# A graph attention layer with a top-2 mixture of experts on one core: GpSimd normalises rows, expert rows are cleared step by step, and the last matrix, the routing and the y store are reordered

## What is computed

```python
def layernorm(x): return (x - mean(x)) / sqrt(var(x) + 1e-5)

q, k, v = (layernorm(x) @ W.T + b for W, b in ((Wq, bq), (Wk, bk), (Wv, bv)))
x = x + softmax(q @ k.T / sqrt(256) + adj + adj) @ v

xf = layernorm(x)
probs = softmax(xf @ router_w + router_b)              # 1354 x 8
topk_p, topk_i = top_k(probs, 2); gates = scatter(topk_p at topk_i)
h = einsum("td,edh->teh", xf, w1) + b1                 # H = 512
gated = silu(h @ wg + bg) * (h @ wv + bv)              # per expert, 512 x 512 each
y = gated @ w2 + b2                                    # 512 x 256 per expert
x = x + einsum("ted,te->td", y, gates)
```

## Time and profile before

| | us |
|---|---|
| median of 3 runs | 450.05 (449.73 to 450.64) |
| the profiled execution | 449.44 |
| its span | 447.7 |

### The profile page before, as it was taken

The page is one execution under the profiler, slowest core; times in us unless marked ns, Lnnn a source line. Parts: engine busy times, 40 slices in busy tenths (PEclk is TensorE's granted clock), DMA queues, the critical chain, the costliest instruction groups (busy, mean ns, idle before and its releaser), DMA issues.

```text
span 447.7 us, 8184 instructions
## 1 busy us (share of the span) xinstructions
PE 390.6 (87%) x2272; PEld 334.7 (75%) x2272; DVE 322.1 (72%) x737; ACT 185.7 (41%) x332; POOL 269.0 (60%) x293
## 2 busy tenths in 40 slices
PE   0887998199999999999999974999888989999981
PEld 0776877089988888988988753788776878888870
DVE  3665879946978988898896987376554756777664
ACT  1574574145455365455545351362222223333320
POOL 3053689835538656755855861666887480377772
PEclk9988999689999999999999996899999999999996
DMA  8761447055666567477266657754564641233235
GB/s 247 259 229 53 141 130 258 33 160 158 208 177 183 190 201 239 145 214 257 98 204 240 266 191 222 280 193 152 215 229 170 245 169 59 84 96 96 68 117 178
DMA packets 44861, 78.94 MB, mean 176 GB/s; under 512 B 5278, under 2 KB 25186, under 8 KB 43796
## 3 DMA queue, kind: packets, MB, share of 16 engines
q1 hardware_dynamic: 32916, 64.87, 43.2%
q10 hardware_dynamic: 9280, 8.00, 5.6%
q0 software_dynamic: 2624, 5.56, 4.1%
HBM read 56.13 MB, written 22.29 MB: 175 GB/s over the span
## 4 chain that ended last, share of the span: by engine, by line
PE 44%; DVE 15%; DMA 14%; issue 9%; POOL 5%; ACT 4%; ACTq 3%; DVEq 2%; SPq 2%; POOLq 1%
PE ps L978 21%; PE ps L1279 9%; DMA expert_out<-ysum 6%; DVE acc L1391 5%; PE ps L1176 4%; DMA xblk<-expert_rows 2%; DMA first_row<-in_L_ffn_bv 2%; DMA wq_raw<-in_L_gnn_Wq 2%; PE ps L1124 2%; PE ps L1178 2%; DVEq L340 2%; DVE ps L1705 2%; POOL picked L704 1%; DMA picked<-expert_out,ypos_i 1%; POOL lo L597 1%
## 5 line engine op out<-in xcount | busy, mean ns | idle before, releaser
L597 POOL TENSOR_TENSOR lo<-raw,hi 128x512 fp32r<-128x512 f32 x60 | 76.0, 1297 | 59.0 <-DVE acc L1391 55.4
L1279 PE MATMUL ps<-weights,bT_hi 128*128 x232 | 72.4, 393 | 0.0
L978 PE MATMUL ps<-hi,w1T_lo 128*128 128x512 f32 x128 | 55.8, 436 | 17.1 <-DVE w1T_lo L1332 10.3
L978 PE MATMUL ps<-hi,w1T_hi 128*128 128x512 f32 x128 | 53.0, 414 | 0.0
L978 PE MATMUL ps<-lo,w1T_hi 128*128 128x512 f32 x128 | 52.6, 411 | 0.0
L1279 PE MATMUL ps<-weights,bT_lo 128*128 x116 | 48.8, 420 | 3.8 <-ACT silu L952 3.1
L1279 PEld LDWEIGHTS ps<-weights,bT_hi 128*128 128x128 f32 x232 | 43.8, 189 | 7.5
L1176 PE MATMUL ps<-v,pT_hi 128*128 128x256 f32 (+3 forms) x242 | 44.7, 286 | 0.0
L978 PEld LDWEIGHTS ps<-hi,w1T_lo 128*128 128x128 f32 x128 | 25.8, 202 | 23.0 <-DVE w1T_lo L1332 10.5
L1279 PE MATMUL ps<-weights,gT_hi 128*128 x232 | 42.9, 283 | 0.0
L1391 DVE SCALAR_TENSOR_TENSOR acc<-raw,b1T,acc 128x512 f32<-128x512 f32 x48 | 41.4, 862 | 1.5
(11 more groups left out here) (222 smaller groups left out, 994.5 us busy)
## 6 DMA issues: line engine op xcount, KB each, us to landing
raw<-in_L_ffn_wg SPq DMA_DIRECT2D x8, 1024.0 KB, 6.3
raw<-in_L_ffn_wv SPq DMA_DIRECT2D x8, 1024.0 KB, 6.5
products<-ring SPq DMA_DIRECT2D x28, 256.0 KB, 4.0
landed<-products SPq DMA_DIRECT2D x7, 1024.0 KB, 7.2
adj_sb<-in_adj SPq DMA_DIRECT2D x10, 677.0 KB
bias<-biases SPq DMA_DIRECT2D x8, 640.0 KB, 5.5
w1raw<-in_L_ffn_w SPq DMA_DIRECT2D x8, 512.0 KB, 5.1
landed<-in_L_ffn_w SPq DMA_DIRECT2D x8, 512.0 KB, 4.2
```

The source lines that it names most:

```text
L597: G.tensor_tensor(lo[j % RAWS][:, k, :], raw[j % RAWS][:, k, :], r32(hi[j % HIS][:, k, :]), ALU.subtract).then_inc(m_lo, 1)
L978: last = nc.tensor.matmul(o, a, b, start=begins and n == 0, stop=ends and n == len(m) - 1)
L1279: last = nc.tensor.matmul(o, stationary[i][:, k, :], part(e, ats[j] + k * width, width), start=n == 0, stop=n == len(m) - 1)
```

## The change

What it does, in the order of the program:
- The factors of all tiles are computed in one go on VectorE after all statistics. Rows of tiles 0 and 1 stay on ScalarE, those of tiles 2 to 10 go to GpSimd. The rest of `wqk` is computed ahead of the tile loop, one `turn_w1` stands ahead of the wait for it. SyncE waits for the query and key matrices before it loads w1 and raw. `gather_bias(0)` is in one piece and `multiply(0, 0)` goes chunk by chunk.
- `gather_bias(3)` stands inside step 1, behind the first two rests of the transposed probabilities; the load of `first_row` 4 stands behind a raw load. L1549 is a TENSOR_SCALAR in place of a TENSOR_TENSOR. GpSimd adds the value bias to x one tile a step. The copy of the normalised tile (`xn2_copy`) is gone, TensorE reads it where it is.
- In each of the eleven steps SyncE clears 128 rows of each of the eight experts (1 MB); the eight clears after the steps are gone, and a scatter waits for its step's clear.
- The bias sums of matrices 14 and 15 are split and begun earlier, matrix 15's ahead of the last `add_mix`; its lo is made by GpSimd (two chunks) and by VectorE ahead of the tables; routing and ranking stand elsewhere between the product chunks; block 0 is loaded from row 0 without the table; VectorE's rest of block 0 stands inside the tables.
- In an expert block ScalarE copies gT before it stores y and loads rows; y sums have three buffers in place of two.

```diff
-    ROWS = 4
+    ROWS, YSUMS = 4, 3
...
-    FACTORS = [(0, 2 * PER), (2 * PER, TILES - 2 * PER)]
+    FIRST = 2
...
+            sp.wait_ge(wqk_in, 48)
             load_w1(0)
             load_raw(0)
             load_first_row(0)
...
+            def clear_rows(t):
+
+                if t > 0:
+                    sp.wait_ge(rows_cleared, 16 * t)
+                sp.dma_start(xs.rearrange("(e c p) d -> p c e d", e=E, p=P)[:, t, :, :],
+                             zeros[:, :].rearrange("p (a d) -> p a d", a=1).broadcast_to([P, E, D])
+                             ).then_inc(rows_cleared, 16)
...
-                if s + 4 < MATS:
+                if 0 < s and s + 4 < MATS:
                     load_first_row(s + 4)
                 store_product(2 * j + 1)
                 if j + RAWS < MATS:
                     load_raw(j + RAWS)
+                if s == 0:
+                    load_first_row(s + 4)
...
+                if s < TILES:
+                    clear_rows(s)
...
-            sp.wait_ge(ends_done, 1)
-            clear_ends(0, padded[0])
-            clear_ends(E // 2, padded[1])
             load_bias(0)
+            load_weights(2)
+            load_down(2)
             store_bias_row(TILES + 3)
             store_product(2 * TILES + 6)
+
+            sp.wait_ge(scattered, 16 * TOPK * TILES)
+            sp.dma_start(xblk[:, 0, :], xs[0:P, :]).then_inc(rows_in[0], 16)
             store_product(2 * TILES + 7)
-            sp.wait_ge(padded[0], 16 * (E // 2))
             sp.wait_ge(rows_done, 1)
-            sp.wait_ge(scattered, 16 * TOPK * TILES)
-            for i in range(3):
+            for i in range(1, 3):
                 row = sp.value_load(at(block_row[0:1, :], i), min_val=0, max_val=E * REGION - P)
                 sp.dma_start(xblk[:, i, :], xs[bass.ds(row, P), :]).then_inc(rows_in[i], 16)
-            load_weights(2)
-            load_down(2)
             load_bias(1)
             store_product(2 * MATS - 2)
+            store_bias_row(MATS - 1)
             load_bias(2)
             store_product(2 * MATS - 1)
-            store_bias_row(MATS - 1)
             sp.wait_ge(tables_done, 1)
             for e in range(SLOTS, E):
...
+                pool.wait_ge(rows_cleared, 16 * (t + 1))
...
-            finish_factors(pool.wait_ge, G, 1, pool)
+            def x_rows(t):
+                w = width(t)
+                G.tensor_scalar(xn2_all[:w, t, :], x1[:w, t, :], rs[:w, 1, t:t + 1], rs[:w, 3, t:t + 1],
+                                ALU.mult, ALU.add).then_inc(xn_last_done, 1)
+
+            pool.wait_ge(factors_done, 1)
+            for t in range(FIRST, TILES):
+                x_rows(t)
...
-            for t in range(TILES):
+            for t in range(2):
...
+                if s + 1 < TILES:
+                    add_bv(s + 1)
                 if 0 <= s - 4:
                     count_tile(s - 4)
                     scatter(s - 4)
             count_tile(TILES - 3)
-            scatter(TILES - 3)
+
+            pool.wait_ge(m_hi, MATS)
+            pool.wait_ge(acc_done, KH * (MATS - 1) + 2)
+            for k in range(2):
+                chunk_lo(MATS - 1, k)
             count_tile(TILES - 2)
-            scatter(TILES - 2)
-            scatter(TILES - 1)
-            sum_lo(MATS - 1)
...
+            product_lo(0)
             pool.wait_ge(tables_done, 1)
-            for e in range(E):
+            down_lo(0)
+            for e in range(1, E):
...
-            x_rows(0)
-            x_rows(1)
+            for t in range(FIRST):
+                x_rows(t)
             act.wait_ge(small_done, 1)
             copy(wvT[0][:, :, D:VW], bk_turned[:, :, :]).then_inc(wvT_hi, 1)
-            x_hi(0)
-            x_rows(2)
-            x_hi(1)
             act.wait_ge(wqk_mm, 1)
             copy(wqk[0][:, :, :], ps[:, 4:7:2, 0:D]).then_inc(wqk_hi, 1)
-            x_rows(3)
+            x_hi(0)
+            x_hi(1)
             for t in range(TILES):
                 if t + 2 < TILES:
                     x_hi(t + 2)
                 v_part(t)
-                if t + 4 < TILES:
-                    x_rows(t + 4)
                 if t == 2:
-                    w1_hi(0, 0, 4)
-                    w1_hi(0, 1, 5)
+                    w1_hi(0, 0, 5)
+                    w1_hi(0, 1, 4)
...
-                if s == 1:
-                    sum_hi(3)
                 keep_bias_row(j, MIX)
                 matrix_hi(s + 3)
                 keep_product(2 * j)
                 pT_part(s - 1, 2)
                 if s + 1 < TILES:
                     q_part(s + 1)
-                if 0 <= s - 2:
-                    xn2_copy(s - 2)
+                if s == 1:
+                    sum_hi(3)
                 sum_hi(s + 3)
                 w1_hi(j // 2 + 1, j % 2, COMB)
                 if s < TILES:
                     probabilities(s)
+                else:
+                    xn2T_part(TILES - 2)
                 keep_product(2 * j + 1)
...
-            xn2T_part(TILES - 2)
             matrix_hi(MATS - 1)
+            xn2T_part(TILES - 1)
             keep_bias_row(LATE, MIX)
-            xn2_copy(TILES - 1)
             w1_hi(LATE // 2 + 1, LATE % 2, COMB)
-            xn2T_part(TILES - 1)
+            keep_product(2 * LATE)
             sum_hi(MATS - 1)
-            keep_product(2 * LATE)
+            keep_product(2 * LATE + 1)
             down_hi(0)
-            keep_product(2 * LATE + 1)
             keep_bias_row(LATE + 1, MIX)
             slot_hi(1)
             keep_product(2 * LATE + 2)
             down_hi(1)
+            keep_product(2 * LATE + 3)
...
+                if 0 <= s - 1 < BLOCKS:
+                    act.wait_ge(gT_mm, s)
+                    if s >= 3:
+                        act.wait_ge(y_mm, s - 2)
+                    copy(gT[(s - 1) % 2][0][:, :, :], by_k(ps[:, BANK_GT[(s - 1) % 2], :], KH)).then_inc(gT_hi, 1)
                 if 0 <= s - 3 < BLOCKS:
                     b = s - 3
                     act.wait_ge(y_sum, b + 1)
                     if b > 0:
                         act.wait_ge(y_out, 16 * b)
-                    act.dma_start(ys[span(b, P), :], ysum[:, b % 2, :]).then_inc(y_out, 16)
+                    act.dma_start(ys[span(b, P), :], ysum[:, b % YSUMS, :]).then_inc(y_out, 16)
                 if s + 3 < BLOCKS:
                     load_rows(s + 3)
-                if 0 <= s - 1 < BLOCKS:
-                    act.wait_ge(gT_mm, s)
-                    if s >= 3:
-                        act.wait_ge(y_mm, s - 2)
-                    copy(gT[(s - 1) % 2][0][:, :, :], by_k(ps[:, BANK_GT[(s - 1) % 2], :], KH)).then_inc(gT_hi, 1)
...
-                pe.wait_ge(xn_done, t + 1)
-                if t >= 2:
+                if t < FIRST:
+                    pe.wait_ge(xn_done, t + 1)
+                else:
+                    pe.wait_ge(xn_last_done, t - FIRST + 1)
                     pe.wait_ge(xT_lo, t - 1)
...
-                pe.wait_ge(m_lo, KH * (j + 1))
+                pe.wait_ge(m_lo, KH * j + chunks[-1] + 1)
...
+                    turn_w1(0, 0, 5)
                     pe.wait_ge(wqk_lo, 1)
-                    turn_w1(0, 0, 4)
-                    turn_w1(0, 1, 5)
+                    turn_w1(0, 1, 4)
                 if t == 3:
                     queries(0)
                 if t == 6:
-                    multiply(0, 0)
+                    for k in range(KH):
+                        multiply(0, 0, range(k, k + 1))
...
             route(TILES - 2)
+            turn_xn2(TILES - 1)
             multiply(LATE, 0, range(KH // 2))
-            turn_xn2(TILES - 1)
+            route(TILES - 1)
             multiply(LATE, 0, range(KH // 2, KH))
             rank(TILES - 2)
-            route(TILES - 1)
-            multiply(LATE, 1)
+            multiply(LATE, 1, range(KH - 1))
             rank(TILES - 1)
+            multiply(LATE, 1, range(KH - 1, KH))
...
+            pe.wait_ge(prod_done, 2 * LATE + 1)
+            for k in range(KH):
+                multiply(LATE + 2, 0, range(k, k + 1))
             pe.wait_ge(bias_row_done, LATE + 2)
             sum_bias(LATE + 2, MIX)
-            pe.wait_ge(prod_done, 2 * LATE + 1)
-            multiply(LATE + 2, 0)
...
-            statistics(0)
-            statistics(1)
-            rough_factors(0)
-            finish_factors(dve.wait_ge, V, 0, dve)
+            for g in range(len(GROUPS)):
+                statistics(g)
+            factors()
...
+            dve.wait_ge(wqk_hi, 1)
+            sub(wqk[1][:, :, :], ps[:, 4:7:2, 0:D], r32(wqk[0][:, :, :])).then_inc(wqk_lo, 1)
             for t in range(TILES):
                 if t + 2 < TILES:
                     x_rest(t + 2)
                 v_rows(t)
-                if t == 0:
-                    statistics(2)
-                    rough_factors(1)
                 if t == 1:
-                    dve.wait_ge(wqk_hi, 1)
-                    sub(wqk[1][:, :, :], ps[:, 4:7:2, 0:D], r32(wqk[0][:, :, :])).then_inc(wqk_lo, 1)
```

(48 more changed lines are left out.)

101 lines of the change are left out of this document (43 added, 58 removed).

## The result

The changed kernel takes 442.43 us (median of 4 runs, 441.74 to 442.77) against 450.02 for the kernel before; the ratio is 0.9828, 95% interval 0.9811 to 0.9845. The forecast was 425.6, with 415 to 437: the sign was right, the gain 7.6 us where 24.4 were forecast. The gain is clear of the noise, but under 2%. The profiled execution has a span of 439.8 us (before 447.7).

A forecast was written before the change was run, and what follows sets the result against it. TensorE alone was taken to bound the nine steps, so gains lie in holes outside them: 7 + 9.4 + 0 + 3 + 5 = 24.4 off 449.4, plus 0.6 for the median: 425.6 us, range 415 to 437.

The forecast's parts named there:

- the factors then end at 13.57 + 1.4 = 15.0: First stage: adding the third group's statistics on VectorE delays all row factors by 1.4 us, to 15.0.
- the four bias sums are issued together: First stage: helps remove TensorE's 2.85 us wait for GpSimd's lo of the first matrix; VectorE's longer block costs some 0.7.
- rival D: Step 1: another wait, the query rest and then the residual sum, replaces L1549's; 3 us earned, not 9.4; 432; chance 0.1.
- short hole: Step 1: a short TensorE wait ahead of the product's second half at 80.0, partly half clock, ending at 83.5.
- rival E: Nine steps: the 1 MB clears make them DMA-bound if each costs above 9.3 us; say 453; chance 0.03.
- rival C: After the steps: the first row of matrix 15 isn't held, so no 5 us TensorE stand; 420.5; chance 0.15.
- GpSimd now issues three tiles' back to back, until 269.9: After the steps: GpSimd's last scatters, three tiles' in a row, are all issued by 269.9, ahead of the first block's load.
- landing 5 later: After the steps: the last scatters land 5 us after issue, and the first block is then loaded, at 277.7.
- VectorE's remaining tables: After the steps: 4.4 us of tables behind VectorE's new wait for the first block, behind the lower bound of -3.
- Rivals A: First stage: GpSimd's new burst blocks VectorE's 0.15 us bias instruction until 24 to 26; stage -1, not 7; 433.6; chance 0.14.
- B: Expert blocks: the store reordering earns nothing, as the row loads behind the stores become late; 431; chance 0.12.
- F: First stage and end: chunked product and early rest find other operands late; together they earn 2; 433.5; chance 0.06.

The follow-up runs named there:

- the seven repairs: Changed kernel with third-group statistics and matrix 0's bias sums split, matrix 4's first row loaded earlier, plus the four repairs behind the steps: 428.61 us, ratio 0.9559.
- the four repairs: Changed kernel with matrix 15's first bias sums, third expert's weights and VectorE's first-block lo later, third-last tile's scatter earlier: 436.99 us, ratio 0.9729.

## Why the prediction was wrong

**First stage, 7 forecast, 0.8 measured.** The step that failed is "the factors then end at 13.57 + 1.4 = 15.0". It counted the added work and took its data as there. In the kernel before, the statistics of the third group ran at 20.29, and no row told when that part of x had landed; it was 12.04, with VectorE idle ahead. The trace of before held a hint: its statistics start at 5.3 and 8.6 us, each released by the landing of its group, so an estimate by the same spacing puts the third group at 11.9. The wait was to be "just covered" up to 16.3; the factors came at 16.64, and the half clock made 1.3 us late into 4.1 by 24.5. The run with the statistics split off gives 5.0 for this cause. The second failure is "the four bias sums are issued together" booked as a gain for the product with 0.7 us of cost; three of them ran at 1.37 us each beside GpSimd, and splitting them gave 2.7. The two don't add up to 7.7, as GpSimd's lo is then the next wait. That GpSimd's rows are hidden was right.

**Step 1, 9.4 forecast, 6.0 measured.** The form of L1549 was right (0.21 us in all steps). The forecast's times are on the clock of the kernel before, 0.8 us later than this trace's; on it the row landed at 72.9 (72.5 forecast), which was right, VectorE's sum behind it ended at 78.4 (76.7), the second half began at 81.6 (80.0) and ended at 86.9 (83.5). So two terms were too small: the sum, whose four instructions took 5.5 us beside GpSimd's subtraction where the forecast left 4.2, and the "short hole", which was 4.67 us, with half clock behind it in all twelve matmuls. The forecast also booked the gain on L1549 alone. In the kernel before that edit alone meets rival D; what cleared the way was spreading the additions beside it, which the forecast had costed as GpSimd's slack and nothing else: 4.1 us in step 1 without it, 12.3 with it. With matrix 4's row in time the changed kernel's step 1 earns 11.3 us, more than was forecast.

**Nine steps, 0 forecast, -0.9.** The 1 MB clears are hidden, as the share of 0.79 (from 0.59) shows; rival E is out. The loss is one wait of 1.1 us for the place of a tile, near 226.

**After the steps, 3 forecast, -3.0.** The hole behind the last mix was forecast at about 5 us, with its cause, and is 5.16 and 5.2 to 7.5 in all kernels that kept it as it was; rival C is out. Here the forecast's clock is 5.9 us later than this trace's. On it TensorE went on at 255.5 (255.1 forecast), ended the first half of product 15 at 276.6 (273.9), GpSimd ended the last scatter at 274.9 (269.9), and the first block came at 282.6 (277.7). The step that failed is thus "GpSimd now issues three tiles' back to back, until 269.9": they ended 5.0 us later. The count that releases them waits for TensorE, which was late itself: the half clock behind the 5.16 us hole, to 256.9, was not in the sum (TensorE is 2.9 us less ahead at 255.6 than at 249.59, part of it the 0.97 us wait for the last tile, which was forecast at 1.3). The term "landing 5 later" held, with 5.6; but 2.4 of that is the third expert's loads, moved ahead of the blocks' in the same diff, as the run without them shows (4.57 us from issue to landing for 6.99). The forecast told of the loads that leave SyncE's queue and not of those that enter it. The hole ahead of the first block was therefore 5.92, and not "as wide as that before 279.83", 3.2. The scatter moved ahead of the count takes 1.8 off it. How the 5.0 us divide between the half clock and the order of instructions on GpSimd stays open. "VectorE's remaining tables", kept as a bound, lie in the 1.1 us lost at the second block, 0.55 of which came back when they were moved.

**Expert blocks, 5 forecast, 5.0 measured** from the same cut at 284.40, or 6.1 from the first turn of gated rows. Right, by the mechanism that was given, as the y store alone shows, with one turn at 6.27 us where none above 6 was expected. Rivals A (0.15 us for bqk_each, at 17.46) and B (waits for row loads behind the first block 1.8 us, as before) are out. F is what happened at the start and the end in effect, and worse than F priced it: the two earned -2.2 where F has 2, with a chance of 0.06 that was too small.

In one sentence, the holes of before were costed as gone, and of the waits that take their place only those with a row in the trace of before got a price. With the seven repairs the kernel takes 428.6, three above the forecast; that the time comes so near is in part luck, since it holds waits that the forecast didn't have (the largest 4.15 us) and gains in step 1 above what was forecast.

## What to carry over

When work moves ahead of a wait, ask when its data lands and not only how long it runs; a trace in which it ran late doesn't show that in its own row. When a hole is taken out, lay out the next two instructions of each engine that feeds it: here 10.26 us in step 1 left 4.67, and 2.85 ahead of the first product left 1.98. Keep the half clock behind a new hole as a bound of its own: behind the holes of 4.67 and 5.16 us it cost an estimated 2.4 (twelve matmuls, 0.43 and not 0.23 us apart) and 2 to 3 us, but behind holes of about 1.8 us it came in some executions (granted 0.55 behind the one before 23.41 in the kernel before) and not in others (1.00 behind the same hole with L1549 and the additions edited, and in step 1 with matrix 4's row in time). When a stage is laid out on the clock of the kernel before, compare it on that clock. Where an edit frees one instruction from another engine's burst, look what stands behind it in the queue: shortening the burst earned more than freeing the one.

## What the hardware did that was not expected

A VectorE instruction can be held through a whole run of GpSimd instructions, and not only L1549: the 128x256 TENSOR_TENSOR of the query rest took 10.22 us (0.39 to 1.6 otherwise), and a 74x2 CAST with one operand 2.80 us (2.81 in the run with the four repairs, 0.16 to 0.57 otherwise), until GpSimd's run of instructions ended, to 0.3 us. But a 128x512 SCALAR_TENSOR_TENSOR in such a run took 1.37 us for 0.75, and wasn't held; nor was the 128x2 TENSOR_TENSOR of bqk_each, 0.15 us amid GpSimd's nine rows. What decides between the two wasn't found. The prediction gave the rule of the Trainium skill (SBUF - State Buffer, section "Who interferes with whom") for instructions with at most one SBUF input without its condition: it holds outside the modes in which VectorE uses both port pairs, and the page names cast among the operations that can enter them. Whether this CAST did, no run here shows.

GpSimd's TENSOR_SCALAR with two per-row operands took 0.54 us for 128x256, where the row of the end stage had 0.95.

TensorE was at half clock behind the wait for wq_raw, 5.5 to 6.6 us, in every kernel. With the turns on time it left it between 15.9 and 17.2 in four kernels, but in one with the same instructions there only at 24.3, after 12.4 us of matmuls without a wait. The cause stays open.
